# Attention prologue of a fused AdaLN + attention + MoE kernel: the second head's projections into PSUM banks 4 to 7, half of the third head's ahead of the first scores, the modulation rows' products first

## The chip, the cores and the metric

One Trainium2 chip, one core of it. The metric is device time in microseconds (us) from one launch to its end; lower is better. The inputs and outputs are fp32. A row of the trace gives times from the start of the profiled span.

## The reference, cut to what matters

```python
mod = (_silu(L0_c) @ L0_wmod).reshape(L0_c.shape[0], 6, 1, -1)
sa, ca, ga, sb, cb, gb = (mod[:, 0], mod[:, 1], mod[:, 2], mod[:, 3], mod[:, 4], mod[:, 5])
ga = (2 * (ga >= 0) - 1) * jnp.maximum(jnp.abs(ga), 0.25)   # the same for gb
h = _layernorm(x, axis=-1) * (1 + ca) + sa
x = x + ga * attention(h)          # 16 heads of 128, q and k RMS-normed, rope, softcap, causal
h = _layernorm(x, axis=-1) * (1 + cb) + sb
x = x + gb * moe(h)                # 64 experts, top 6, capacity 96, and a shared expert
```

x is 4 x 512 x 256 (batch, tokens, model). For each batch b and head n the attention makes q, k, v = h @ w, scores, their softmax, the product with v, and the output projection.

## The kernel before

Each engine has a program of its own, written out in order by hand; semaphores tie them together. The attention runs over 4 batches x 16 heads as 64 *periods*. In `period(b, p)` TensorE (PE) does: `scores(b, p)`; the transposes of the head before's output (`o_t`); the transposes of q and k of head p + 1 (`qk_t`); the projections q, k, v of head p + 2 (`qkv`); the output projection of head p - 1 (`proj`); and the product of the probabilities with v of head p (`pv`). So a head's projections are made two periods ahead of its scores. Every fp32 product of the projections and scores is made of three matmuls on split operands (high x high, high x low, low x high): `wh`, `wl` are the halves of a head's weights, `hth`, `htl` those of the transposed h, `qth`, `qtl`, `kth`, `ktl` those of q and k, `oth`, `otl` those of a head's output. ScalarE (ACT) makes the high halves, VectorE (DVE) the low ones.

PSUM has 8 banks. `qkv` writes banks 0 to 3 (one bank for 128 tokens, 384 columns: q, k, v); `qk_t` writes banks 2 and 3; `scores` write banks 4 to 6; `pv` writes banks 7 and 6; `proj` banks 4 and 5. The trace calls all of PSUM `ps` and most SBUF scratch `arena`.

After `qkv` of a head, and before PE can transpose that head's q, a chain over three engines has to run: ACT squares q and k (`take`, L593), DVE sums the squares (`squares_sum`, L861), GpSimd (POOL) raises the mean to the power -1/2 (`norms`, L500 and L502), DVE scales q (`q_scale`, L866). In `take` ACT also copies k and v out of PSUM; after it `weights_high` makes the next head's `wh`, which DVE's `weights_low` follows with `wl`.

Before the first period stands a prologue, with this order on PE: four columns of the modulation (L1282), the transposes of the normalised x (`h1_t`, L1297), `qkv(0, 0)` (24 matmuls, L1313 and L1325), `qk_t(0, 0)` (L1334, L1337), `qkv(0, 1)` (24 matmuls, L1325), `mod_rows` (the other four modulation vectors as rows: four fp32 products of a 128 x 4 stationary tile with 512 columns, which the trace shows as 8 records, L1289), a wait for the loads of the output weights and the gate, and then `period(0, 0)`. DVE copies the rows of `mod_rows` to SBUF (`rows_out`, L855), and reworks them in periods 0 and 1 (`rows_signed`, `rows_clamped`: sign, floor of 0.25). `scores(0, 0)` may write bank 6 only after that copy. The modulation weights for `mod_rows` come with the transfer issued at L337. All loads are issued from one queue (SP) at the start.

## Time and profile before

| | |
|---|---|
| median of 3 runs | 1035.48 us (1033.2 to 1037.18) |
| profiled execution, its own time | 1035.61 us |
| its span | 1033.8 us |
| PE busy | 979.1 us, 95% of the span |
| DVE, ACT, POOL busy | 692.0, 589.1, 383.3 us |
| mean granted clock of TensorE | 0.975 of full speed |

The span is what the trace covers; about 1.8 us of the execution's own time lie around it. A busy PE says that matmuls were in flight, not that they ran at full speed. TensorE has two clock levels, 1.2 and 2.4 GHz; the granted clock is given as a share of the higher.

### The profile page before, as it was taken

The numbers are of one execution on the slowest core, as the hardware profiler recorded it, in microseconds if no ns is written. First come the engines' busy times: TensorE is split into PE (matmuls) and PEld (weight loads), VectorE is DVE, ScalarE is ACT, GpSimd is POOL, SyncE is SP. The second block draws the span as 40 slices with busy tenths as digits, with TensorE's granted clock in tenths as the row PEclk, the third lists the DMA queues.
The fourth block names the chain that finished last, engine by engine and source line by source line (L and its number), as shares of the span: only waits on it lengthen the run. The fifth ranks groups of instructions, "written<-read, shape, count | busy, mean of one in ns | idle before, by whom it ended". The sixth has DMA issues, their size and how long they took to land.

```text
span 1033.8 us, 18164 instructions
## 1 busy us (share of the span) xinstructions
PE 979.1 (95%) x6301; PEld 874.2 (85%) x6301; DVE 692.0 (67%) x1783; ACT 589.1 (57%) x1093; POOL 383.3 (37%) x454
## 2 busy tenths in 40 slices
PE   4999999999999999999999999999989789999982
PEld 4899999999999999999999999999855356666661
DVE  3666666778788876878888686888568123324646
ACT  2666766766676676667666766666531024444420
POOL 3222222223322564332256432225624515555460
PEclk9999999999999999999999999999999899999985
DMA  9995000000100110010011004000261049999847
GB/s 349 333 325 209 0 0 1 1 2 14 45 1 1 49 49 33 5 53 1 2 48 39 24 2 145 2 1 17 100 204 36 26 121 309 311 313 306 235 46 243
DMA packets 71213, 103.42 MB, mean 100 GB/s; under 512 B 10237, under 2 KB 52352, under 8 KB 70750
## 3 DMA queue, kind: packets, MB, share of 16 engines
q1 hardware_dynamic: 45854, 74.62, 22.2%
q0 software_dynamic: 11808, 12.87, 6.1%
q10 hardware_dynamic: 13472, 14.90, 4.7%
q8 instruction: 46, 0.75, 0.3%
q14 instruction: 33, 0.27, 0.1%
HBM read 68.13 MB, written 40.88 MB: 105 GB/s over the span
## 4 chain that ended last, share of the span: by engine, by line
PE 88%; DVE 5%; DMA 3%; issue 2%; ACT 1%; POOL 0%; SPq 0%; ACTq 0%; POOLq 0%; DVEq 0%
PE ps L1325 26%; PE ps L1378 14%; PE ps L1351 12%; PE ps L1366 9%; PE ps L1531 7%; PE ps L1546 5%; PE ps L1358 3%; PE ps L1334 3%; PE ps L1415 3%; PE ps L1337 3%; PE ps L1484 1%; PE ps L1524 1%; DMA acc<-wos,arena 1%; DMA arena<-slot_rows 1%; PE ps L1538 1%
## 5 line engine op out<-in xcount | busy, mean ns | idle before, releaser
L617 ACT ACTIVATE prob<-ps,rn 128x512 f32<-128x512 f32 (+3 forms) x256 | 121.5, 528 | 113.8 <-PE ps L1351 107.0
L1325 PE MATMUL ps<-wl,hth 128*128 128x384 f32 x512 | 173.1, 338 | 0.0
L1325 PE MATMUL ps<-wh,htl 128*128 128x384 f32 x512 | 172.7, 337 | 0.0
L1325 PE MATMUL ps<-wh,hth 128*128 128x384 f32 x496 | 171.9, 347 | 0.0
L861 DVE TENSOR_REDUCE ss<-arena 128x8 f32<-128x1024 f32 x64 | 78.2, 1221 | 117.1 <-ACT arena L593 117.0
L1378 PE MATMUL ps<-vx,prob 128*128 128x129 f32 (+1 forms) x1280 | 153.4, 274 | 0.2 <-POOL prob L511 0.2
L1378 PEld LDWEIGHTS ps<-vx,prob 128*128 128x128 f32 x1280 | 148.2, 191 | 0.6 <-POOL prob L511 0.6
L593 ACT ACTIVATE arena<-ps 128x1024 f32<-128x1024 f32 x64 | 65.7, 1026 | 119.0 <-PE ps L1325 119.0
L508 POOL TENSOR_SCALAR_AFFINE_SELECT prob<-prob 128x384 f32<-128x384 f32 x64 | 35.6, 557 | 256.2 <-ACT prob L623 256.2
L572 POOL DMA_INDIRECT acc<-wos,arena x64 | 92.8, 1450 | 93.5 <-ACT wos L737 50.3
L517 POOL DMA_INDIRECT slot_rows<-pay,arena x96 | 99.8, 1039 | 43.2 <-issue 24.7
L502 POOL TENSOR_TENSOR rn<-rtmp,neghalf 128x8 f32<-128x8 f32 x64 | 105.4, 1648 | 5.3
L1325 PEld LDWEIGHTS ps<-wl,hth 128*128 128x128 f32 x512 | 97.5, 190 | 0.9 <-issue 0.9
L1325 PEld LDWEIGHTS ps<-wh,htl 128*128 128x128 f32 x512 | 97.2, 190 | 0.0
L1325 PEld LDWEIGHTS ps<-wh,hth 128*128 128x128 f32 x496 | 93.9, 189 | 0.1
L500 POOL TENSOR_SCALAR rtmp<-ss 128x8 f32<-128x8 f32 x64 | 12.6, 197 | 211.3 <-DVE ss L861 211.3
L1351 PE MATMUL ps<-qth,kth 128*128 128x512 f32 (+3 forms) x256 | 87.8, 343 | 0.0
L623 ACT ACTIVATE prob<-prob 128x1280 f32<-128x1280 f32 x64 | 83.7, 1308 | 0.0
L1351 PE MATMUL ps<-qtl,kth 128*128 128x512 f32 (+3 forms) x256 | 82.7, 323 | 0.0
L1351 PE MATMUL ps<-qth,ktl 128*128 128x512 f32 (+3 forms) x256 | 82.4, 322 | 0.0
L1208 DVE TENSOR_TENSOR xn<-ps,arena 96x176 f32<-96x176 f32 x64 | 21.5, 337 | 85.0 <-PE ps L1531 47.8
L891 DVE TENSOR_TENSOR arena<-ps,arena 128x512 f32<-128x512 f32 x118 | 75.6, 681 | 2.2 <-PE ps L1366 2.2
(208 smaller groups left out, 2237.8 us busy)
## 6 DMA issues: line engine op xcount, KB each, us to landing
acc<-pay SPq DMA_DIRECT2D x4, 2048.0 KB, 17.1
wge<-in_wgu SPq DMA_DIRECT2D x20, 352.0 KB
slot_rows<-pay SPq DMA_DIRECT2D x1, 6456.0 KB, 35.8
warena<-acc SPq DMA_DIRECT2D x12, 512.0 KB
arena<-slot_rows ACTq DMA_DIRECT2D x56, 100.9 KB
warena<-in_wqkv SPq DMA_DIRECT2D x1, 4992.0 KB, 20.6
arena<-in_wgu SPq DMA_DIRECT2D x14, 352.0 KB
late_t<-in_wd ACTq DMA_DIRECT2D x14, 192.0 KB
```

Source lines behind the costliest of these rows:

```text
L502: pool.tensor_tensor(rn[:, bass.ds(head(n), 1), :].squeeze(1), rtmp[:], neghalf[:], ALU.pow).then_inc(s["r_rdy"], 1)
L517: pool.indirect_dma_start(buf_d, bass.IndirectOffsetOnAxis(ap=sloti[:, i * K + k:i * K + k + 1], axis=0), pay[:, i, :], None, bounds_check ...
L572: pool.indirect_dma_start(acc_d[acc_of(e)], bass.IndirectOffsetOnAxis(ap=tokc[:, e % TR:e % TR + 1], axis=0), orow[e % ORING], None, bound ...
L617: act_(prob[:, OFF[j]:OFF[j] + w], sflat[:, OFF[j]:OFF[j] + w], ACT.Tanh, scale=rn[:, bass.ds(head(n), 1), TT + j:TT + j + 1].squeeze(1)). ...
L623: act_(prob[:, 0:1280], prob[:, 0:1280], ACT.Exp, scale=CAP).then_inc(s["expd"], 1)
L861: nc.vector.tensor_reduce(ss[:].rearrange("p (c i) -> p i c", c=2), sq, X, ALU.add).then_inc(s["ss_rdy"], 1)
L891: tt(ya, yp, ya, ALU.add).then_inc(s["y_added"], 1)
L1325: last = mm(ps[:, i, 0:3 * DH], hp[:, k, i * P:(i + 1) * P], wp[:, k, :], start=(k == 0 and m == 0), stop=(k == KC - 1 and m == 2))
L1351: last = mm(sflat[:, OFF[j]:OFF[j] + w], kp[:, j * P:(j + 1) * P], qp[:, T - w:T], start=(m == 0), stop=(m == 2))
L1366: last = mm(yps[:, i, :], op[:, i * P:(i + 1) * P], wp[:], start=(m == 0), stop=(m == 2))
L1378: last = mm(o, prob[:, c:c + P], vx[:, bass.ds((vslot(n) * TT + j) * (DH + 1), DH + 1)], start=(j == 0), stop=(j == i))
L1531: last = mm(ps[0:C, 1 + e % 2, 0:2 * M], xgt[:, e % 2, k, :], wgus[e % RING][:, k, :], start=(k == 0), stop=(k == KC - 1))
```

## The change

The prologue is put in another order, and the second head (`is_second`: batch 0, head 1) gets places of its own.

- PE: `mod_rows` moves from behind `qkv(0, 1)` to ahead of `qkv(0, 0)`. `qkv(0, 1)` writes banks 4 to 7 (`qbank`), so it no longer waits for head 0's q, k and v to be taken out of banks 0 to 3, and stands ahead of `qk_t(0, 0)`. It waits for the copy of the modulation rows (banks 6 and 7), and `scores(0, 0)` now waits until head 1's q and v have left banks 4 to 7. The first two token tiles of `qkv(0, 2)` stand ahead of `period(0, 0)`, the other two stay inside it. The wait for the output weights and the gate moves behind `period(0, 0)`.
- ACT: the high halves of the second head's weights (`second_high`) are made early, into the places of `oth` and `otl`, which are free then. `weights_high(0, 2)` follows `take(0, 0)`. `qk_high(0, 0)` moves inside `take(0, 1)`, behind its square.
- DVE: `second_low` makes the low halves into `kth` and `ktl`; `rows_out`, `rows_signed` and `rows_clamped` all come ahead of `squares_sum(0, 0)`; `squares_sum(0, 1)` comes ahead of `qk_t(0, 0)`.

No arithmetic is added or left out, except that one pass over a head's weights (high, and low) is two passes of half the size for head 1.

```diff
--- before.py
+++ after.py
@@ -236,6 +236,8 @@
         oth = hb("oth", [P, T])
         otl = hb("otl", [P, T])
         heads.close()
+        wh1 = [oth, otl]
+        wl1 = [kth, ktl]
         late_gu = [sb("late_h", [P, KC * T]), sb("late_l", [P, KC * T]), sb("late_wh", [P, KC * 3 * DH]), sb("late_wl", [P, KC * 3 * DH])]
         late_wd = [sb(f"late_t{i}", [P, T]) for i in range(6)]
 
@@ -318,6 +320,14 @@
 
         def vslot(n):
             return n % 4
+
+        def is_second(b, n):
+
+            return isinstance(b, int) and isinstance(n, int) and b == 0 and n == 1
+
+        def qbank(b, n):
+
+            return SB if is_second(b, n) else 0
 
         SB = 4
 
@@ -590,11 +600,14 @@
                 a.wait_ge(s["qkv_rdy"], cnt(b, n))
                 if some(cnt(b, n - 1)):
                     a.wait_ge(s["ss_rdy"], cnt(b, n - 1))
-                act_(sq, ps[:, 0:TT, 0:2 * DH].rearrange("p i (c d) -> p i c d", c=2), ACT.Square).then_inc(s["squared"], 1)
-                act_(kr, ps[:, 0:TT, DH:2 * DH], ACT.Copy).then_inc(s["k_copied"], 1)
+                q0 = qbank(b, n)
+                act_(sq, ps[:, q0:q0 + TT, 0:2 * DH].rearrange("p i (c d) -> p i c d", c=2), ACT.Square).then_inc(s["squared"], 1)
+                if is_second(b, n):
+                    qk_high(0, 0)
+                act_(kr, ps[:, q0:q0 + TT, DH:2 * DH], ACT.Copy).then_inc(s["k_copied"], 1)
                 dst = vx[:, bass.ds(vslot(n) * TT * (DH + 1), TT * (DH + 1))].rearrange("p (i d) -> p i d", i=TT)[:, :, 0:DH]
                 a.wait_ge(s["ones_rdy"], 1)
-                act_(dst, ps[:, 0:TT, 2 * DH:3 * DH], ACT.Copy).then_inc(s["v_copied"], 1)
+                act_(dst, ps[:, q0:q0 + TT, 2 * DH:3 * DH], ACT.Copy).then_inc(s["v_copied"], 1)
 
             def h_high(b):
 
@@ -606,9 +619,17 @@
 
             def weights_high(b, n):
 
-                if some(cnt(b, n - 1)):
+                if isinstance(b, int) and isinstance(n, int) and (b, n) == (0, 2):
+                    a.wait_ge(s["qkv_rdy"], cnt(0, 0))
+                elif some(cnt(b, n - 1)):
                     a.wait_ge(s["qkv_rdy"], cnt(b, n - 1))
                 act_(wh[:], wq[:, :, bass.ds(head(n), 1), :].squeeze(2), ACT.Copy).then_inc(s["wh_rdy"], 1)
+
+            def second_high():
+
+                for k in range(KC):
+                    ins = act_(wh1[k][:, 0:3 * DH], wq[:, k, 1, :], ACT.Copy)
+                ins.then_inc(s["wh_rdy"], 1)
 
             def cap(b, n):
 
@@ -679,13 +700,12 @@
 
             a.wait_ge(s["ld_wq0"], 16)
             weights_high(0, 0)
+            second_high()
             h_high(0)
             take(0, 0)
-            weights_high(0, 1)
+            weights_high(0, 2)
             a.wait_ge(s["g_rdy"], 4)
-            qk_high(0, 0)
             take(0, 1)
-            weights_high(0, 2)
             a.wait_ge(s["ld_wqkv"], 16)
             for p in range(2):
                 period(0, p)
@@ -819,6 +839,13 @@
                 v.wait_ge(s["wh_rdy"], cnt(b, n))
                 tt(wl[:], wq[:, :, bass.ds(head(n), 1), :].squeeze(2), wh[:].bitcast(F32), ALU.subtract).then_inc(s["wl_rdy"], 1)
 
+            def second_low():
+
+                v.wait_ge(s["wh_rdy"], 2)
+                for k in range(KC):
+                    ins = tt(wl1[k][:, 0:3 * DH], wq[:, k, 1, :], wh1[k][:, 0:3 * DH].bitcast(F32), ALU.subtract)
+                ins.then_inc(s["wl_rdy"], 1)
+
             def x_attended(b):
 
                 v.wait_ge(s["y_added"], 2 * cnt(b, H - 1))
@@ -863,7 +890,8 @@
             def q_scale(b, n):
                 v.wait_ge(s["r_rdy"], cnt(b, n))
                 v.wait_ge(s["v_copied"], cnt(b, n))
-                tt(qn, ps[:, 0:TT, 0:DH], rn[:, bass.ds(head(n), 1), 0:TT].squeeze(1).unsqueeze(2).to_broadcast([P, TT, DH]), ALU.mult).then_inc(s["q_scaled"], 1)
+                q0 = qbank(b, n)
+                tt(qn, ps[:, q0:q0 + TT, 0:DH], rn[:, bass.ds(head(n), 1), 0:TT].squeeze(1).unsqueeze(2).to_broadcast([P, TT, DH]), ALU.mult).then_inc(s["q_scaled"], 1)
 
             def qk_t(b, n):
                 v.wait_ge(s["qth_rdy"], cnt(b, n))
@@ -1022,8 +1050,6 @@
                     qk_t(b, p + 1)
                 if some(cnt(b, p - 1)):
                     wo_low(b, p - 1)
-                if not has_before(b) and isinstance(p, int) and p < 2:
-                    rows_signed() if p == 0 else rows_clamped()
                 if isinstance(p, int) and has_before(b):
                     if p == 1:
                         x_attended(b - 1)
@@ -1087,14 +1113,16 @@
             ts(g[:], g[:], qkws[:, 0:1], DH ** -0.5 / CAP, ALU.mult, ALU.mult).then_inc(s["g_rdy"], 1)
             v.wait_ge(s["g_rdy"], 4)
 
+            second_low()
+            rows_out()
+            rows_signed()
+            rows_clamped()
             squares_sum(0, 0)
+            weights_low(0, 2)
             q_scale(0, 0)
-            weights_low(0, 1)
+            squares_sum(0, 1)
             qk_t(0, 0)
-            squares_sum(0, 1)
-            rows_out()
             q_scale(0, 1)
-            weights_low(0, 2)
             v.wait_ge(s["consts"], 10)
             cp(trir[:], tri[:]).then_inc(s["pos_w"], 1)
             ts(onesr[:], tri[:], 0.0, 1.0, ALU.mult, ALU.add).then_inc(s["pos_w"], 1)
@@ -1297,9 +1325,15 @@
                         last = pe.transpose(ps[:, bank + k, i * P:(i + 1) * P], src[:, i, k * P:(k + 1) * P], ident[:])
                 last.then_inc(s["xt_ps"], 1)
 
-            def qkv(b, n):
-
-                before = cnt(b, n - 1)
+            def qkv(b, n, tiles=(0, TT)):
+
+                before = 0 if is_second(b, n) else cnt(b, n - 1)
+                q0 = qbank(b, n)
+                whs, wls = ([m[:, 0:3 * DH] for m in wh1], [m[:, 0:3 * DH] for m in wl1]) if is_second(b, n) else ([wh[:, k, :] for k in range(KC)], [wl[:, k, :] for k in range(KC)])
+                if is_second(b, n):
+                    pe.wait_ge(s["rows_sb"], 1)
+                if tiles == (0, 2):
+                    before = cnt(b, n - 2)
                 if some(before):
                     pe.wait_ge(s["v_copied"], before)
                     pe.wait_ge(s["q_scaled"], before)
@@ -1310,21 +1344,22 @@
                         for k in range(KC):
                             if i == 0:
                                 pe.wait_ge(s["h_high"], KC * (b + n // H) + k + 1)
-                            mm(ps[:, i, 0:3 * DH], hth[:, k, i * P:(i + 1) * P], wh[:, k, :], start=(k == 0), stop=False)
+                            mm(ps[:, q0 + i, 0:3 * DH], hth[:, k, i * P:(i + 1) * P], whs[k], start=(k == 0), stop=False)
                     pe.wait_ge(s["ht_rdy"], KC * (b + n // H + 1))
                 pe.wait_ge(s["wl_rdy"], cnt(b, n))
-                for i in range(TT):
+                for i in range(*tiles):
                     if i == 2 and some(before):
                         pe.wait_ge(s["qt_rdy"], before)
                     if i == 3 and some(before):
                         pe.wait_ge(s["kt_rdy"], before)
                     for k in range(KC):
-                        for m, (hp, wp) in enumerate(((hth, wh), (hth, wl), (htl, wh))):
+                        for m, (hp, wp) in enumerate(((hth, whs), (hth, wls), (htl, whs))):
                             if first and i < 2 and m == 0:
                                 continue
-                            last = mm(ps[:, i, 0:3 * DH], hp[:, k, i * P:(i + 1) * P], wp[:, k, :],
+                            last = mm(ps[:, q0 + i, 0:3 * DH], hp[:, k, i * P:(i + 1) * P], wp[k],
                                       start=(k == 0 and m == 0), stop=(k == KC - 1 and m == 2))
-                last.then_inc(s["qkv_rdy"], 1)
+                if tiles[1] == TT:
+                    last.then_inc(s["qkv_rdy"], 1)
 
             def qk_t(b, n):
 
@@ -1340,13 +1375,14 @@
             def scores(b, n):
                 pe.wait_ge(s["qt_rdy"], cnt(b, n))
                 pe.wait_ge(s["kt_rdy"], cnt(b, n))
+                if isinstance(b, int) and isinstance(n, int) and (b, n) == (0, 0):
+                    pe.wait_ge(s["v_copied"], cnt(0, 1))
+                    pe.wait_ge(s["q_scaled"], cnt(0, 1))
                 for j, w in ((0, 512), (1, 384), (3, 128), (2, 256)):
                     if j < 2 and some(cnt(b, n - 2)):
                         pe.wait_ge(s["y_added"], 2 * cnt(b, n - 2) + (j - 1))
                     if j == 2 and some(cnt(b, n - 1)):
                         pe.wait_ge(s["o_normed"], 2 * cnt(b, n - 1))
-                    elif j == 2:
-                        pe.wait_ge(s["rows_sb"], 1)
                     for m, (kp, qp) in enumerate(((kth, qth), (kth, qtl), (ktl, qth))):
                         last = mm(sflat[:, OFF[j]:OFF[j] + w], kp[:, j * P:(j + 1) * P], qp[:, T - w:T], start=(m == 0), stop=(m == 2))
                     if j != 1:
@@ -1438,7 +1474,7 @@
                         pe.wait_ge(s["ld_sh"], 32)
                     shared_up(p - (H - 2))
                 if not (is_last(b) and static and p >= H - 2):
-                    qkv(b, p + 2)
+                    qkv(b, p + 2, (2, TT) if static and b == 0 and p == 0 else (0, TT))
                 if static and p == 4 and has_before(b):
                     pe.wait_ge(s["h2s_rdy"], b)
                 if static and p == 5 and has_before(b):
@@ -1453,14 +1489,15 @@
                 pv(b, p)
 
             h1_t(0)
+            mod_rows()
             qkv(0, 0)
+            qkv(0, 1)
             qk_t(0, 0)
-            qkv(0, 1)
-            mod_rows()
+            qkv(0, 2, (0, 2))
+            period(0, 0)
             pe.wait_ge(s["ld_wo"], 16)
             pe.wait_ge(s["ld_gate"], 16)
-            for p in range(2):
-                period(0, p)
+            period(0, 1)
             with pe.Fori(2, SIDE) as p:
                 period(0, p)
             for b in range(B - 1):
```

PE's program at the start, where the prologue's large pieces stand (arena in the first row is the modulation weights, sc the activated condition; hth and wh are head 0's operands). Before:

```order
L1297 MATMUL ps<-ident,xn 128x128 [waits xn_rdy,consts]
...
L1313 MATMUL ps<-wh,hth 128x384 [waits h_high,wh_rdy]
...
L1334 MATMUL ps<-ident,arena 128x128 [waits v_copied,q_scaled]
...
L1325 MATMUL ps<-wh,hth 128x384 [waits wl_rdy,q_scaled,v_copied]
...
L1289 MATMUL ps<-arena,sc 4x512 [waits ld_wmod2]
...
L1351 MATMUL ps<-qth,kth 128x512 [waits qt_rdy,kt_rdy,ld_gate,ld_wo]
```

Of the changed kernel (oth and kth are here the high and low half of head 1's weights):

```order
L1325 MATMUL ps<-ident,xn 128x128 [waits xn_rdy,consts]
...
L1317 MATMUL ps<-arena,sc 4x512 [waits ld_wmod2]
...
L1347 MATMUL ps<-wh,hth 128x384 [waits h_high,wh_rdy]
...
L1359 MATMUL ps<-oth,hth 128x384 [waits wl_rdy,rows_sb]
...
L1369 MATMUL ps<-ident,arena 128x128 [waits v_copied,q_scaled]
...
L1359 MATMUL ps<-wh,hth 128x384 [waits wl_rdy,q_scaled,v_copied]
...
L1387 MATMUL ps<-qth,kth 128x512 [waits v_copied,q_scaled,kt_rdy,qt_rdy]
```

The rows' products stand ahead of everything of head 0, head 1's projections ahead of head 0's transposes, and the first scores wait for head 1's chain too.

DVE's program between the last small product of the prologue and head 1's scaling. Before:

```order
L861 TENSOR_REDUCE ss<-arena 128x4x2
L866 TENSOR_TENSOR arena<-ps,rn 128x512
L820 TENSOR_TENSOR wl<-warena,wh 128x768
L870 TENSOR_TENSOR qtl<-ps,qth 128x512
L872 SCALAR_TENSOR_TENSOR ktl<-ps,g,kth 128x512
L861 TENSOR_REDUCE ss<-arena 128x4x2
L855 COPY arena<-ps 4x1024
L866 TENSOR_TENSOR arena<-ps,rn 128x512
```

Of the changed kernel:

```order
L846 TENSOR_TENSOR kth<-warena,oth 128x384
L846 TENSOR_TENSOR ktl<-warena,otl 128x384
L882 COPY arena<-ps 4x1024
L1033 TENSOR_SCALAR arena<-arena 4x256
...
L1043 SCALAR_TENSOR_TENSOR arena<-arena 4x2x256
L888 TENSOR_REDUCE ss<-arena 128x4x2
L840 TENSOR_TENSOR wl<-warena,wh 128x768
L894 TENSOR_TENSOR arena<-ps,rn 128x512
L888 TENSOR_REDUCE ss<-arena 128x4x2
L898 TENSOR_TENSOR qtl<-ps,qth 128x512
L900 SCALAR_TENSOR_TENSOR ktl<-ps,g,kth 128x512
L894 TENSOR_TENSOR arena<-ps,rn 128x512
```

The copy and the rework of the modulation rows moved ahead of head 0's sum of squares, and head 1's sum ahead of head 0's low halves.

## Rows read from the trace of the kernel before

**Rows 1.** The page: busy time of each engine

```profile
PE 979.1 (95%) x6301; PEld 874.2 (85%) x6301; DVE 692.0 (67%) x1783; ACT 589.1 (57%) x1093; POOL 383.3 (37%) x454
```

**Rows 2.** PE's waits from 40 to 700 us: total, times, longest

```profile
PE ps L1378 <- POOL prob L511: 0.2, 1, 0.2
```

**Rows 3.** PE's waits from 0 to 46 us

```profile
PE ps L1282 <- DMA arena<-in_wmod: 6.5, 1, 6.5
PE ps L1334 <- DVE arena L866: 5.2, 1, 5.2
PE ps L1313 <- ACT hth L605: 2.0, 1, 2.0
```

**Rows 4.** PE's timeline: start, length, line, operands, idle before

```profile
10.17 1.94 PE L1297 MATMUL ps<-ident,xn 128*128 128x128 f32 x8
14.10 1.95 PE L1313 MATMUL ps<-wh,hth 128*128 128x384 f32 x4 [1.99 <-ACT hth L605]
...
18.41 0.52 PE L1325 MATMUL ps<-wh,hth 128*128 128x384 f32 x1
18.73 0.52 PE L1325 MATMUL ps<-wl,hth 128*128 128x384 f32 x1
...
19.69 0.38 PE L1325 MATMUL ps<-wl,hth 128*128 128x384 f32 x1
...
26.50 1.06 PE L1334 MATMUL ps<-ident,arena 128*128 128x128 f32 x4 [5.18 <-DVE arena L866]
...
32.17 0.33 PE L1325 MATMUL ps<-wh,hth 128*128 128x384 f32 x1
32.35 0.33 PE L1325 MATMUL ps<-wl,hth 128*128 128x384 f32 x1
...
33.31 3.60 PE L1289 MATMUL ps<-arena,sc 128*4 128x512 f32 x8
36.84 0.50 PE L1351 MATMUL ps<-qth,kth 128*128 128x512 f32 x1
```

**Rows 5.** The chain that ended last: head 0's scaling

```profile
21.36 1.03 ACT arena L593
...
22.48 1.23 DVE ss L861
...
24.07 1.65 POOL rn L502
...
25.75 0.70 DVE arena L866
```

**Rows 6.** SP's timeline and L337's own view: issue, then DMA to landing

```profile
3.10 0.61 SPq L337 DMA_DIRECT2D arena<-in_wmod  x1
...
DMA to landing us min/median/max: 10.3/10.3/10.3
```

**Rows 7.** PE's timeline at the end; a window there (clock third from the end)

```profile
1000.48 13.99 PE L1573 MATMUL ps<-pay,warena 64*128 64x256 f32 x32 [3.65 <-DVE pay L1263]
...
1010.00:1012.00 2.00, 2.00 (x6) 1.63 (x5) 0.00 (x0) 0.00 (x0) 0.00 (x0) 0.50 1.07 378
```

**Rows 8.** Windows: the clock (third number from the end) after the wait

```profile
27.00:28.00 1.00, 1.00 (x7) 1.00 (x6) 0.31 (x1) 0.34 (x1) 0.00 (x0) 0.50 1.17 377
30.00:31.00 1.00, 1.00 (x8) 1.00 (x7) 0.00 (x0) 0.00 (x0) 0.00 (x0) 0.99 1.00 426
```

**Rows 9.** DVE's timeline

```profile
22.48 1.22 DVE L861 TENSOR_REDUCE ss<-arena 128x8 f32<-128x1024 f32 x1 [6.43 <-ACT arena L593]
...
36.95 1.21 DVE L855 COPY arena<-ps 4x1024 f32<-4x1024 f32 x1 [1.25 <-PE ps L1289]
...
52.84 1.01 DVE L1015 SCALAR_TENSOR_TENSOR arena<-arena 4x512 f32<-4x512 f32 x1
```

**Rows 10.** The chain that ended last: the first period

```profile
40.22 0.71 ACT kth L642
...
44.42 2.50 PE ps L1378 x20
```

## The prediction

> **What bounds the kernel now.** I read the page's busy times first: PE is busy for 979.1 of 1033.8 us, DVE for 692.0, ACT for 589.1 [rows 1]. So PE is the engine to watch, and the question is where it waits. The view of waits, asked for PE alone, answers it: from 40 to 700 us PE waited once, for 0.2 us [rows 2]. What the change touches lies ahead of that, and there PE waited three times: 6.5 us for the first modulation weights, 2.0 us for the first high half of h, and 5.2 us for head 0's scaled q [rows 3]. Since PE is gapless behind the prologue, a microsecond won or lost before the first scores comes out at the end nearly whole: the time at which `scores(0, 0)` starts, 36.84 us [rows 4], is the number that the whole prediction turns on. I call it S.
>
> The timeline of PE shows a second thing: its speed. A 128x384 matmul follows the one before it after 0.32 us at 18.41 us (half speed) and after 0.18 us at 32.17 us (full speed) [rows 4]. The change of pace stands at 19.69 us, 5.6 us after the projections started at 14.10. The wait of 5.2 us cost more than itself: the granted clock is 0.50 at 27 us and back at 0.99 in the stretch from 30 us, 3.5 us after PE resumed at 26.50 [rows 8, 4]. (For the first 19 us the spacing, not the granted clock, tells the level: 384 columns in 0.32 us are 1.2 GHz.)
>
> **The change part by part.**
>
> *The rows' products, moved.* Before, the 8 records take 33.31 to 36.84, 3.5 us at full speed [rows 4]. Now they stand behind the transposes, which end at 12.1 us (10.17 + 1.94), and wait for the transfer issued at 3.10, which lands 10.3 us later, at 13.4 us [rows 4, 6]. There PE runs at half speed. The price at 1.2 GHz comes from the kernel's end, where 32 records of 256 columns take 13.99 us at granted clock 0.50, 0.437 us each [rows 7]; records of 512 columns are twice that, and 8 of them 7.0 us. So they end at 20.4 us, where `qkv(0, 0)` had begun at 14.10: the start is 6.3 us later, against 3.5 us taken out further on. That is a loss of 2.8 us, unless the clock rises while they run.
>
> *Does it?* This decides the case. At the kernel's end PE ran 14 us without a gap on stationary tiles of 64 rows, and the clock stayed at 0.50 all the time [rows 7]. From 14.10 us and from 26.50 us, on tiles of 128 x 128, it rose after 5.6 and 3.5 us. The stationary tile of the rows' products has 4 columns of 128; it is further from the tiles that brought the clock up than the tile that didn't. So I take it that the clock stays at 1.2 GHz through them, and keep the other answer as a rival.
>
> *`qkv(0, 0)`.* 24 matmuls, starting cold at 20.4. Before, they took 7.2 us (14.10 to 21.3) with the clock rising 5.6 us in. If it rises 3.5 us in, as after the later wait, 2.1 us of half speed (6.5 matmuls of 0.32) become 6.5 x 0.175 = 1.1 us, so 6.3 us. I take the middle, 6.8: end at 27.2 (26.7 to 27.6).
>
> *`qkv(0, 1)` in the 5.2 us wait.* It now follows at once, warm: 24 x 0.175 = 4.2 us, end at 31.4. Its operands are early: two half passes of high weights cost ACT at most twice the 1.03 us of its 1024-column square [rows 5], and PE now asks for ACT's high half of h 6.3 us later than before; the low ones lie in DVE's idle 6.43 us ahead of its first sum [rows 9]. Its wait for the copied rows ends at 20.4 + 1.2 = 21.6. The PE wait it fills is not the end of the wait: `qk_t(0, 0)` may start 5.2 us after 27.2 (the chain is 1.03, 1.23, 1.65 and 0.70 us and the hand-overs [rows 5]), so at 32.4, with 1.0 us of idle PE left. Since PE no longer stands for 5.2 us in a row, the second fall of the clock goes. What that fall cost, 26.50 to 30.0 at half speed, is 3.5 / 2 = 1.75 us.
>
> *The wait comes back behind head 1.* `scores(0, 0)` needs banks 4 to 7 free, and they are free when head 1's chain is through. That is another 5.2 us, after 31.4: S = 36.6. In it PE has 8 transposes (1.94 us at half speed [rows 4], so 1.0) and 12 matmuls of head 2 (2.1) to do; they end at 32.4 + 3.1 = 35.5, and PE idles 1.1 us. On ACT, the high half of head 0's k and the copies of head 1's k and v now stand between head 1's square and the release of v. At 0.71 us each, as that high half [rows 10], they follow the transposes' end at 33.4 and are done at 35.5; the power of head 1 is ready 4.4 us after 31.4 (as 25.72 came after 21.3 [rows 5]), at 35.8. So the chain sets S, and they don't, by 0.3 us. On DVE, `weights_low(0, 2)` now stands ahead of `q_scale(0, 0)`. It waits for ACT's square, two copies and a 768-column pass (at most 1.03 + 1.42 + 1.03 = 3.5) and is no longer than the 1.23 of a sum: 4.7 us at the very most against 4.4, so at worst 0.3 us on head 0's chain. The wait for the output weights and the gate, now behind period 0, held PE for nothing before: the rows' products run up to 36.84 [rows 4].
>
> *Half of head 2 early.* It takes 2.1 us out of period 0, but does that move anything? In period 0, `pv(0, 0)` starts 7.6 us after the scores (36.84 to 44.42) and the chain through it is not PE's but tanh, high halves, the load of the exponential's table, exponential and mask [rows 10]. In the chain of what ended last, PE's own projections of that period do not appear. So the 2.1 us turn into idle PE, in front of tile 2 (which needs the low half of head 1's q) or of `pv`. I cost the piece at a gain of 0.1 us, since head 2's chain can start a little sooner, and at no more than 0.3 us, the size of the wait that remained ahead of `pv`.
>
> *DVE's rows first.* The copy is 1.21 us and the longest of the five reworks 1.01 [rows 9]; even at that all six are under 6.3 us, and they run from 20.4 to 26.7 at the latest. Head 0's square is done at 27.2 + 1.1 = 28.3. In periods 0 and 1 DVE is the lighter by the same work, and PE did not wait for it there [rows 2]: nothing.
>
> **The sum.** S goes from 36.84 to 36.6, and 0.1 us comes from period 0: a gain of 0.3 us. Over the two bounds of the clock's rise, S is 36.1 to 37.0, a gain of 0.8 to a loss of 0.1. Against the profiled execution's own time of 1035.61 that is 1035.3; this execution is 0.13 us above the median of 1035.48, so I say 1035.2. Three runs of one kernel lie 4.0 us apart, which is far more.
>
> **The rivals.**
>
> *The clock rises inside the rows' products.* What speaks for it is that PE is busy without a gap from 13.4 on. With the rise 3.5 to 5.6 us in, half (3.5 of 7.0) to four fifths of them are done cold and they end at 18.7 to 19.7; `qkv(0, 0)` is warm, 4.2 + 0.2, so 23.0 to 24.0; `qkv(0, 1)` 27.2 to 28.2; S = 32.4 to 33.4. (DVE, with its rows done 6.3 us after 18.7 at the latest, might cost 0.9 of that.) Gain 3.4 to 4.4, in the middle 3.9, with period 0 4.0: 1031.5 us. The Trainium skill, page "TensorE: Matmul & The Clock Gate", section "What's actually happening", says that the gate follows how busy PE has lately been, whatever it works on; by that rule this rival is the forecast. The stretch of 14 us above does not agree with it.
>
> *Slower: the clock stays low past the projections.* PE now has idle stretches of 1.0 and 1.1 us where it was gapless after 26.50. If PE stays at half speed until the first scores are done, `qkv(0, 0)` takes 7.7 (S + 0.9), `qkv(0, 1)` 7.7 instead of 4.2 (+ 3.5), and the scores, of 3840 columns or ten times 384, 10 x 0.145 more (+ 1.5): 5.9 us against the gain of 0.3, 1041 us. It decides "slower" only from a rise behind S; a rise at the end of `qkv(0, 1)` is a loss of 4.1 us and still no difference. Against it: both rises before came 3.5 and 5.6 us after 128 x 128 matmuls began.
>
> *The transfer is late.* Each us by which the second modulation weights land after 13.4 moves S by one; before, PE asked for them at 33.3 and they had 20 us of slack. To lose over 0.5% they must land 5.5 us later. Nothing in the issue order changes, so I give it little.
>
> *Nothing is gained since the wait only moves.* This is near the forecast: without the clock effect, S would be within 0.3 us of before by coincidence of a loss of 2.8 and the gains of the filled wait.
>
> **How the numbers follow.** 0.5% is 5.2 us, about what a measurement of this kernel can tell from no change, and more than the forecast or the first rival reach. Chances: forecast 0.55; clock rising inside the rows' products 0.33; clock low for longer 0.05; late transfer 0.02; something unseen 0.05, either way. Faster by over 0.5% takes the first rival's far end and a before that ran high: 0.08. Slower by over 0.5%: 0.06. Within: 0.86. The range reaches down to the first rival (1031.5) less 1 us of the runs' scatter, and up by the forecast's loss plus the 2 us by which runs lie over their median: 1030.5 to 1038.0. The forecast's own is 1033.0 to 1037.5.
>
> **What would show it.** In the changed kernel's trace: the rows' products start at 13.4 and end at 20.4, each record starting 0.87 us after the last (0.43 us in the later ones would be the rival); spacing of 0.32 us in the first half of `qkv(0, 0)`; no granted clock of 0.50 after it; PE idle about 1.0 us ahead of head 0's transposes, 1.1 ahead of the scores, and some 2.3 in all within period 0; S at 36.6. Wrong it would be by a clock that rises early, or by a wait in ACT's or DVE's new order that I took to be covered.

## The result and the profile after

| | before | changed |
|---|---|---|
| median of 5 runs | 1036.81 us (1033.2 to 1037.67) | 1028.23 us (1027.1 to 1029.77) |
| profiled execution, its own time | 1035.61 us | 1028.68 us |
| its span | 1033.8 us | 1026.8 us |
| mean granted clock | 0.975 | 0.977 |

The ratio is 0.9929, 95% interval 0.9915 to 0.9943: the changed kernel is faster by 0.7%, some 7.4 us. The forecast was 1035.2 us with a range of 1030.5 to 1038.0, and a chance of 0.08 for a gain over 0.5%. It was wrong.

The page of the changed kernel, its span and its busy times, answers to [rows 1]:

```profile
span 1026.8 us, 18168 instructions
...
PE 975.8 (95%) x6301; PEld 870.5 (85%) x6301; DVE 692.2 (67%) x1784; ACT 589.1 (57%) x1094; POOL 384.9 (37%) x454
```

PE is busy for 3.3 us less (979.1 to 975.8) on the same work, so part of the gain must be pace, not waiting. PE's waits of the changed kernel from 0 to 42 us (in total, times, longest; from 42 to 700 us there is none) answer to [rows 3]:

```profile
PE ps L1310 <- DMA arena<-in_wmod: 6.4, 1, 6.4
PE ps L1317 <- DMA arena<-in_wmod: 1.5, 1, 1.5
PE ps L1359 <- DVE qtl L898: 1.4, 1, 1.4
PE ps L1387 <- DVE arena L894: 1.1, 1, 1.1
PE ps L1369 <- DVE arena L894: 0.9, 1, 0.9
PE ps L1414 <- POOL prob L521: 0.8, 1, 0.8
```

The wait of 5.2 us is gone, and that of 2.0 us for h has become one of 1.5 us for the modulation weights; 0.9, 1.1, 1.4 and 0.8 have come. Where the time came from stands in PE's timeline of the changed kernel, which answers to [rows 4] (start, length, operands, idle before):

```profile
10.09 1.94 PE L1325 MATMUL ps<-ident,xn 128*128 128x128 f32 x8
13.52 4.98 PE L1317 MATMUL ps<-arena,sc 128*4 128x512 f32 x8 [1.49 <-DMA arena<-in_wmod]
18.43 0.98 PE L1347 MATMUL ps<-wh,hth 128*128 128x384 f32 x4
19.25 0.34 PE L1359 MATMUL ps<-wl,hth 128*128 128x384 f32 x1
...
22.72 0.33 PE L1359 MATMUL ps<-oth,hth 128*128 128x384 f32 x1
...
27.99 0.66 PE L1369 MATMUL ps<-ident,arena 128*128 128x128 f32 x4 [0.95 <-DVE arena L894]
...
32.29 0.47 PE L1387 MATMUL ps<-qth,kth 128*128 128x512 f32 x1 [1.08 <-DVE arena L894]
...
36.70 0.41 PE L1359 MATMUL ps<-wh,hth 128*128 128x384 f32 x1 [1.38 <-DVE qtl L898]
...
39.83 2.50 PE L1414 MATMUL ps<-vx,prob 128*128 128x129 f32 x20 [0.79 <-POOL prob L521]
```

The rows' products took 4.98 us, not 7.0 (all at 1.2 GHz) and not 3.5 (all at 2.4). Within them the pace doubled: cold for x us and warm for the rest is x + (7.0 - x) / 2 = 4.98, so x = 3.0. `qkv(0, 0)` follows at full pace from its first record, 18.43 to 22.72, 4.3 us. S, the start of the first scores, is 32.29.

From one span to the other it is 7.0 us. S accounts for 4.55 (36.84 to 32.29), the stretch from S to `scores(0, 2)` for 0.36 (21.23 to 20.87), so 4.9 are there by the third head. Of the rest, 0.9 stands ahead of the last output projection (its idle time is 2.39 us before and 1.46 after), and 1.0 between the second layer's transposes and the first expert (67.4 and 66.35 us). The further traces below tell against the change as the cause of either. The idle time ahead of that projection is 1.46 us in all of them, variants of the kernel before included. The second stretch takes 56.8 or 58.5 us and nothing else, for variants of either kernel (before: 56.8 in the copy, 58.5 with the rows' products moved; changed: 58.5 and 56.8 in two copies). So I take the last 2 us of the pair of profiles for scatter; where its two values come from stands with the copies below. Those executions were on other chips, where the kernel before takes some 1026 us; each ratio below is to runs of the kernel before on the same chip.

### The profile page after: what moved, and what is told of

It is laid out like the page before. It is cut to its first block, busy times and chain, and to the rows that moved or that the text cites. A ratio compares the mean times of both kernels' runs of the same rounds, so it can differ in the third digit from the quotient of the medians.

```text
span 1026.8 us, 18168 instructions
## 1 busy us (share of the span) xinstructions
PE 975.8 (95%) x6301; PEld 870.5 (85%) x6301; DVE 692.2 (67%) x1784; ACT 589.1 (57%) x1094; POOL 384.9 (37%) x454
## 4 chain that ended last, share of the span: by engine, by line
PE 88%; DVE 5%; DMA 4%; issue 1%; ACT 1%; POOL 0%; SPq 0%; ACTq 0%; POOLq 0%; DVEq 0%
PE ps L1359 25%; PE ps L1414 14%; PE ps L1387 12%; PE ps L1402 9%; PE ps L1568 7%; PE ps L1583 5%; PE ps L1451 3%; PE ps L1394 3%; PE ps L1369 3%; PE ps L1372 3%; PE ps L1521 1%; DMA acc<-wos,arena 1%; DMA warena<-acc 1%; PE ps L1561 1%; DMA arena<-in_wmod 1%
## 5 line engine op out<-in xcount | busy, mean ns | idle before, releaser
L1359 PE MATMUL ps<-wh,hth 128*128 128x384 f32 x488 | 168.4, 345 | 1.4 <-DVE qtl L898 1.4
L1359 PE MATMUL ps<-wl,hth 128*128 128x384 f32 x504 | 169.0, 335 | 0.0
L1359 PE MATMUL ps<-wh,htl 128*128 128x384 f32 x504 | 168.8, 335 | 0.0
L604 ACT ACTIVATE arena<-ps 128x1024 f32<-128x1024 f32 x64 | 65.7, 1026 | 116.7 <-PE ps L1359 116.7
L582 POOL DMA_INDIRECT acc<-wos,arena x64 | 95.6, 1493 | 89.4 <-ACT wos L757 57.6
L1359 PEld LDWEIGHTS ps<-wl,hth 128*128 128x128 f32 x504 | 94.8, 188 | 0.9 <-issue 0.9
L1359 PEld LDWEIGHTS ps<-wh,htl 128*128 128x128 f32 x504 | 94.6, 188 | 0.0
L1359 PEld LDWEIGHTS ps<-wh,hth 128*128 128x128 f32 x488 | 91.8, 188 | 1.6 <-issue 1.6
L510 POOL TENSOR_SCALAR rtmp<-ss 128x8 f32<-128x8 f32 x64 | 12.6, 197 | 205.3 <-DVE ss L888 205.3
```

The costliest lines, as they stand in the source:

```text
L582: pool.indirect_dma_start(acc_d[acc_of(e)], bass.IndirectOffsetOnAxis(ap=tokc[:, e % TR:e % TR + 1], axis=0), orow[e % ORING], None, bound ...
L1359: last = mm(ps[:, q0 + i, 0:3 * DH], hp[:, k, i * P:(i + 1) * P], wp[k], start=(k == 0 and m == 0), stop=(k == KC - 1 and m == 2))
```

## The experiments

**The rows' products first, and nothing else.** In the kernel before, moved on PE as shown; DVE's copy of the rows moves ahead of the first sum of squares with them:

```diff
             h1_t(0)
+            mod_rows()
             qkv(0, 0)
             qk_t(0, 0)
             qkv(0, 1)
-            mod_rows()
```

> The kernel before with one part of the change: the rows' products (and their copy on DVE) ahead of qkv(0,0); the rest as before. Theory 1 (the early rows carry the gain: they fill PE's wait for h and bring the clock up before the projections): they run 13.5 to 18.4 us, qkv(0,0) is warm and ends at 22.7, the wait of 5.2 us stays, first scores at 22.7 + 5.2 + 0.9 + 4.2 = 33.0 us if the clock stays up in the wait, 34.7 if it falls: 3.8 or 2.1 us below the kernel before. Theory 2 (the filled wait carries it): first scores at 36 us or later, under 1 us gained.

Measured: 1028.19 against 1025.75 us, ratio 1.0017 (1.0007 to 1.0028). Its timeline (PE), and two windows of it (the clock is the third number from the end):

```profile
13.85 5.02 PE L1289 MATMUL ps<-arena,sc 128*4 128x512 f32 x8 [1.85 <-DMA arena<-in_wmod]
...
28.36 1.12 PE L1334 MATMUL ps<-ident,arena 128*128 128x128 f32 x4 [5.10 <-DVE arena L866]
...
41.24 1.12 PE L1334 MATMUL ps<-ident,arena 128*128 128x128 f32 x4 [3.18 <-DVE arena L866]
```

```profile
28.00:29.00 1.00, 0.65 (x3) 0.65 (x4) 1.00 (x2) 0.00 (x0) 0.00 (x0) 0.50 1.25 450
...
41.00:42.00 1.00, 0.76 (x4) 0.76 (x5) 1.00 (x3) 0.00 (x0) 0.00 (x0) 0.50 1.06 312
```

The products take 5.02 us here too, so the early rise of the clock doesn't need the other edits. But alone the move gains nothing; it loses 0.17%. S is 35.98, later than the 33.0 to 34.7 of the first theory, and from there it goes worse. Before, the products stood between `qkv(0, 1)` and its scaled q and filled that chain; with them gone, PE waits 3.18 us for it inside period 0, and the clock falls a second time. `scores(0, 2)` starts at 61.71 us, against 58.07 and 58.89 in the two traces of the kernel before.

**The rows' products late.** In the changed kernel they go behind the first half of `qkv(0, 2)`, with the waits that banks 6 and 7 then need; DVE copies and reworks the rows where it did before.

```diff
             h1_t(0)
-            mod_rows()
             qkv(0, 0)
             qkv(0, 1)
             qk_t(0, 0)
             qkv(0, 2, (0, 2))
+            mod_rows()
             period(0, 0)
```

> The changed kernel with the rows' products behind the first half of qkv(0,2), as late as before, and everything else of the change kept. Theory 1: qkv(0,0) starts cold at 14.1 and ends at 21.3, qkv(0,1) at 25.5, head 1's chain at 30.7, the rows' products 3.6 us behind it: first scores at 34.3 us, 2 us above the changed kernel. Theory 2 (only the filled wait counts): within 0.5 us of the changed kernel's 32.3.

Measured: 1020.87 against 1025.75 us, 0.9953 (0.9935 to 0.9970). PE's timeline:

```profile
14.01 1.96 PE L1345 MATMUL ps<-wh,hth 128*128 128x384 f32 x4 [1.75 <-ACT hth L618]
...
30.18 3.59 PE L1317 MATMUL ps<-arena,sc 128*4 128x512 f32 x8 [1.05 <-issue]
33.70 0.50 PE L1387 MATMUL ps<-qth,kth 128*128 128x512 f32 x1
```

The products cost 3.59 us warm and start after a stretch idle of 1.05 us that is there in either place. S is 33.70, between the two theories. With them first it is 32.29, 33.45 and 33.91 in three profiles of the changed kernel. So by the traces their place is worth 1.4 us at most and may be worth nothing; the two ratios' intervals (0.9935 to 0.9970 here, 0.9921 to 0.9961 for the copy below) overlap. Most of the gain is there without that edit.

**Half of head 2 not early.** The changed kernel without the `qkv(0, 2, (0, 2))` ahead of period 0:

```diff
             qk_t(0, 0)
-            qkv(0, 2, (0, 2))
             period(0, 0)
...
-                    qkv(b, p + 2, (2, TT) if static and b == 0 and p == 0 else (0, TT))
+                    qkv(b, p + 2)
```

> The changed kernel with qkv(0,2) whole inside period 0. Theory 1, as in the prediction: the first scores stay at 32.3 us, pv(0,0) stays at 39.8 since tanh, table load, exponential and mask set it; within 0.3 us of the changed kernel. Theory 2 (the half is worth its 2.1 us): pv(0,0) at 41 us or later.

Measured: 1024.01 against 1025.75 us, 0.9987 (0.9971 to 1.0004). Some three quarters of the gain go with 12 matmuls that only change places. PE's timeline and windows of this kernel:

```profile
32.93 0.77 PE L1387 MATMUL ps<-qth,kth 128*128 128x512 f32 x1 [3.20 <-DVE arena L894]
```

```profile
30.00:31.00 1.00, 0.00 (x0) 0.00 (x0) 1.00 (x3) 1.00 (x3) 0.77 (x2) 0.88 1.04 442
...
36.00:37.00 1.00, 1.00 (x6) 1.00 (x6) 0.00 (x0) 0.92 (x3) 0.00 (x0) 0.50 1.04 400
...
38.00:39.00 1.00, 1.00 (x8) 1.00 (x7) 0.56 (x1) 0.98 (x3) 0.00 (x0) 1.00 1.03 238
```

S is 32.93, as the forecast's step would have it: the half doesn't move the chain. But PE stands for 3.20 us ahead of it instead of 1.08, the clock falls in that wait (the scores' first record lasts 0.77 us, not 0.47) and is low for 6.8 us. From S to `scores(0, 2)` it takes 23.23 us instead of 20.87, 2.36 us more. The timed difference to the changed kernel is larger, some 4.7 us (0.9987 against 0.9941, each to the kernel before on its own chip); what makes up the rest no run shows.

**The same with work that computes nothing.** Twelve matmuls into a free bank take the half's place in the kernel above (added work, its results unused):

```diff
             qk_t(0, 0)
+            for _ in range(12):
+                mm(ps[:, 0, 0:3 * DH], hth[:, 0, 0:P], hth[:, 1, 0:3 * DH], start=True, stop=True)
```

> The changed kernel without the early half of qkv(0,2), and in its place 12 matmuls of 128x384 whose result nobody reads. Without the half, the clock fell in a wait of 3.2 us and pv(0,0) started 9.5 us after the first scores instead of 7.6. Theory 1 (the early half is worth its holding of the clock, not its work): pv(0,0) starts 7.6 us after the first scores, as in the changed kernel. Theory 2 (its work counts): 9.5 us again, or over 8.5.

Measured, one execution: 1019.31 us beside a median of 1026.01. PE's timeline and a window:

```profile
33.13 0.47 PE L1387 MATMUL ps<-qth,kth 128*128 128x512 f32 x1 [1.09 <-DVE arena L894]
...
40.68 2.50 PE L1414 MATMUL ps<-vx,prob 128*128 128x129 f32 x20 [0.35 <-POOL prob L521]
```

```profile
36.00:37.00 1.00, 1.00 (x8) 1.00 (x7) 0.29 (x1) 1.00 (x3) 0.00 (x0) 1.00 1.05 406
```

The clock stays up, and `pv(0, 0)` comes 7.55 us after S, as in the changed kernel (7.54), where it was 9.48 with the half late. What the half of head 2 is worth is that it keeps PE busy; that it is done early is worth 0.2 us at most (from S to `scores(0, 2)` 21.06 us here, 20.87 in the changed kernel).

**Tiles of 64 rows.** Each of the rows' products is made of two on the first 64 rows, so half of each sum is left out and the count of records is doubled:

```diff
-  last = mm(ps[0:B, 6 + h, :], sc[:, k, :], wmods[:, k, ...], ...)
+  for r in range(2):
+      last = mm(ps[0:B, 6 + h, :], sc[0:64, k, :], wmods[0:64, k, ...], ...)
```

> The changed kernel with each of the four rows' products replaced by two over the first 64 rows only (the other half of each sum is left out): twice the columns streamed, stationary tiles of 64 x 4. It asks whether the rows of a tile decide if the clock comes up. Theory 1 (tiles of 64 rows don't bring it up, as in the 14 us at the kernel's end): 16 records at 0.87 us, 13.5 to 27.5 us, and qkv(0,0) starts cold; first scores at 43 us or later. Theory 2 (being busy is enough): spacing falls from 0.85 to 0.43 us about 3 us in, the products end at 22 us, first scores at 35.8.

Measured, one execution: 1031.72 us beside a median of 1025.75. PE's timeline, and a window of it:

```profile
13.47 13.81 PE L1318 MATMUL ps<-arena,sc 64*4 64x512 f32 x16 [1.24 <-DMA arena<-in_wmod]
27.21 1.65 PE L1348 MATMUL ps<-wh,hth 128*128 128x384 f32 x4
28.65 0.52 PE L1360 MATMUL ps<-wl,hth 128*128 128x384 f32 x1
...
31.92 0.33 PE L1360 MATMUL ps<-wh,hth 128*128 128x384 f32 x1
```

```profile
30.00:31.00 1.00, 1.00 (x5) 1.00 (x4) 0.91 (x2) 0.00 (x0) 0.00 (x0) 1.00 1.00 426
```

16 records in 13.81 us are 0.863 each, the 0.87 of 1.2 GHz, to the end. That it is the clock, and not a slower kind of matmul, shows in what follows on 128 x 128 tiles: records of 0.52 us, every 0.32 us, until the pace changes at 31.5, 4.3 us after these began; from there on they last 0.33. In 13.8 us without a gap the clock did not rise. The granted clock reads 1.00 in the window, where the spacing is that of 1.2 GHz: ahead of its first change in a trace it can't be used.

**The rows' products twice.** The control for it, the same count of records with whole tiles (added work, the second pass writes what the first did):

```diff
-                for h in range(2):
+                for h in (0, 1, 0, 1):
```

> The changed kernel with the rows' products made twice in a row (the second pass writes the same result). Theory 1 (their 128-row tiles bring the clock up, and it then stays up under them): the second pass takes 3.5 us, first scores 3.5 us later than in the changed kernel, at 35.8 to 36.5. Theory 2 (the rise at 16 us came from the transposes ahead, and tiles of 4 columns don't hold the clock): it falls again in them, first scores at 38 us or later.

Measured, one execution: 1021.3 us beside 1026.1. PE's timeline:

```profile
12.70 7.98 PE L1317 MATMUL ps<-arena,sc 128*4 128x512 f32 x16 [0.56 <-DMA arena<-in_wmod]
```

As many records of as many columns, on 128 rows instead of 64: 7.98 us instead of 13.81. The rise comes 2.0 us after the start (14.0 cold, 7.0 warm), and a whole extra pass leaves S at 34.45, within 0.6 us of the changed kernel's latest.

**Both kernels again.** Unchanged copies on another chip, the changed one on a third too.

> The kernel before, unchanged, as a control: a second profile of it. Of the changed kernel's gain, 5.0 us lie ahead of the third head's scores and 2.0 us behind the attention (0.9 us at the last output projection, 1.0 us in the shared expert's stretch). Theory A (those 2.0 us are scatter of the executions or of the chip): on this chip the stretch from the last head's scores to its output projection takes 13.0 us, as in the four kernels profiled here, and 58.5 us from the transposes of h2 to the first expert. Theory B (they come with the kernel's layout): 13.9 us for the first. The first scores start between 35.1 and 37.0 us, by where the clock rises and falls.

> The changed kernel, unchanged, on the chip on which its variants were timed. Theory A: first scores at 32.3 to 33.0 us (the rows' products start 13.5 to 14.1, by the landing of their weights), the gain over the kernel before is the prologue's 4 to 5 us, a ratio of 0.995 to 0.996. Theory B: the whole 7 us again, 0.993.

> The changed kernel once more, beside the version with two more edits, for their difference on one chip. The first scores start at 32.3 to 33.9 us, by the place of the clock's rise in the rows' products; ratio to the kernel before 0.994.

Measured: before 0.9995 (0.9983 to 1.0008); changed 0.9941 (0.9921 to 0.9961) and 0.9943 (0.9931 to 0.9955), 1020.54 against 1026.01 us. The traces differ from the first ones. The changed kernel's timeline on the second chip:

```profile
13.68 6.47 PE L1317 MATMUL ps<-arena,sc 128*4 128x512 f32 x8 [1.66 <-DMA arena<-in_wmod]
...
33.91 0.47 PE L1387 MATMUL ps<-qth,kth 128*128 128x512 f32 x1 [1.11 <-DVE arena L894]
```

Here the rise came 5.9 us after their start instead of 3.0. Over all profiles with the products first, on whole tiles and made once, they took 4.17 to 6.47 us. The kernel before varies as well; its copy's timeline and windows:

```profile
26.15 1.11 PE L1334 MATMUL ps<-ident,arena 128*128 128x128 f32 x4 [5.17 <-DVE arena L866]
```

```profile
28.00:29.00 1.00, 1.00 (x5) 1.00 (x5) 0.81 (x2) 0.69 (x1) 0.00 (x0) 0.50 1.30 453
...
31.00:32.00 1.00, 1.00 (x4) 1.00 (x4) 0.00 (x0) 0.00 (x0) 0.00 (x0) 0.50 1.00 426
...
33.00:34.00 1.00, 1.00 (x7) 0.88 (x6) 0.00 (x0) 0.00 (x0) 0.00 (x0) 1.00 0.85 327
```

After the same wait the clock was low for 6.8 us in all, where [rows 8] had it back at 30. Its S is 37.65.

The copies also show where the two lengths of the stretch behind the attention come from. PE's timeline and a window of the first trace of the changed kernel, then of the copy on the second chip:

```profile
753.44 0.40 PE L1402 MATMUL ps<-woh,oth 128*128 128x256 f32 x1 [1.46 <-DVE otl L905]
754.00:755.00 1.00, 1.00 (x7) 1.00 (x6) 0.97 (x2) 0.00 (x0) 0.00 (x0) 0.50 1.05 351
764.65 1.06 PE L1325 MATMUL ps<-ident,pay 128*128 128x128 f32 x8 [1.12 <-DVE pay L873]
```

```profile
766.28 1.26 PE L1325 MATMUL ps<-ident,pay 128*128 128x128 f32 x8 [2.63 <-DVE pay L873]
768.00:769.00 1.00, 1.00 (x3) 0.77 (x3) 0.00 (x0) 0.60 (x1) 0.00 (x0) 0.50 0.60 210
```

In the first the clock falls at the last output projection, the work behind it is slow, and it fills the wait for the transposes' operand but for 1.12 us. In the copy the clock stays up there, PE waits 2.63 us, and the clock falls behind that wait: the stretch is 1.7 us longer. In all nine traces with 58.5 us this wait is 2.6 to 2.7 us, and in all other traces 1.0 to 1.4.

**The wait filled in the kernel before.** 24 matmuls into a free bank in the 5.2 us (added work, unused):

```diff
             qkv(0, 0)
+            for _ in range(24):
+                mm(ps[:, 5, 0:3 * DH], hth[:, 0, 0:P], hth[:, 1, 0:3 * DH], start=True, stop=True)
             qk_t(0, 0)
```

> The kernel before with 24 matmuls of 128x384 added, whose result nobody reads, between qkv(0,0) and qk_t(0,0), in PE's wait of 5.2 us (4.2 us of extra work, no work moved). Theory 1 (a part of what the wait costs is the clock, which fell in it in both profiles of the kernel before and came back 3.5 to 5.9 us after PE resumed): no granted clock of 0.50 after 20 us, first scores 1.7 to 3 us sooner, at 34.6 to 35.2 us, and the kernel 1.5 to 3 us faster than before though it does more. Theory 2 (the wait costs only its own length): first scores at 36.8 to 37.6 as before, no difference in time.

Measured: 1023.39 against 1026.01 us, 0.9977 (0.9968 to 0.9986). PE's timeline:

```profile
21.40 4.33 PE L1458 MATMUL ps<-hth 128*128 128x384 f32 x24
26.74 0.66 PE L1334 MATMUL ps<-ident,arena 128*128 128x128 f32 x4 [1.01 <-DVE arena L866]
...
32.03 3.60 PE L1289 MATMUL ps<-arena,sc 128*4 128x512 f32 x8
36.09 0.47 PE L1351 MATMUL ps<-qth,kth 128*128 128x512 f32 x1 [0.46 <-DMA wos<-in_wo]
```

The kernel gets 2.4 us faster by doing more. That is the cost of the clock's fall, measured apart from the wait: from `qk_t(0, 0)` to the rows' products it takes 5.29 us, and 6.81 and 7.98 in the two traces of the kernel before. The last row shows something else: with the clock held up the scores are due at 35.63, and wait 0.46 us for the loads. (The trace names the output weights; the gate's load, issued at 23.44, lands 12.6 us later, at 36.0.) In the kernel before the gate's load lands at 35.1 (23.56 + 11.5) and PE asks for it at 36.84. So the wait that "held PE for nothing" was 1.8 us from holding it.

**The wait for the loads put back.** The changed kernel with the two waits ahead of period 0 again:

```diff
             qkv(0, 2, (0, 2))
+            pe.wait_ge(s["ld_wo"], 16)
+            pe.wait_ge(s["ld_gate"], 16)
             period(0, 0)
-            pe.wait_ge(s["ld_wo"], 16)
-            pe.wait_ge(s["ld_gate"], 16)
             period(0, 1)
```

> The changed kernel with PE's wait for the output weights and the gate back ahead of period 0. The prediction costed the moving of this wait at nothing. Theory 1 (nothing only while the scores start late: the weights land at 35 to 36 us, after the changed kernel's first scores): the first scores start at 35 to 36.1 us with an idle of 2 to 4 us ahead of them, in which the clock may fall; 2 to 4 us slower than the changed kernel. Theory 2 (nothing, as predicted): first scores at 32.3 to 33.9, no difference.

Measured: 1026.60 against 1025.71 us, 1.0005 (0.9992 to 1.0018). PE's timeline and two windows:

```profile
36.70 0.76 PE L1387 MATMUL ps<-qth,kth 128*128 128x512 f32 x1 [4.59 <-DMA gates<-in_gate]
```

```profile
34.00:35.00 1.00, 0.00 (x0) 0.00 (x0) 0.00 (x0) 0.00 (x0) 0.00 (x0) 1.00 0.91 344
...
37.00:38.00 1.00, 1.00 (x3) 0.81 (x3) 0.00 (x0) 0.00 (x0) 0.00 (x0) 0.50 1.08 398
```

The gate's load lands at 36.7 us. PE stands 4.59 us instead of 1.09, so S is 36.70 and 3.5 us late. The clock falls too, and from S to `scores(0, 2)` it takes 23.06 us, 2.2 more. The whole gain is gone. Moving this wait is the edit without which the others show nothing.

**Two further steps.** The modulation weights issued ahead of head 0's weights, and ACT's table for the exponential loaded at the end of the prologue; each alone, and both:

```diff
-            sp.dma_start(wq[:, :, 0:nf, :], wqkv[:, :, 0:nf, :]).then_inc(s["ld_wq0"], 16)
             sp.dma_start(wmods[:, :, 2 * D:6 * D], wmod[:, :, 2 * D:6 * D]).then_inc(s["ld_wmod2"], 16)
+            sp.dma_start(wq[:, :, 0:nf, :], wqkv[:, :, 0:nf, :]).then_inc(s["ld_wq0"], 16)
...
             take(0, 1)
+            act_(warm[:], neghalf[:, 0:1], ACT.Exp)
```

> The changed kernel with only the rows' weights loaded ahead of the first heads' weights. The rows' products start at 12.1 us without a wait; first scores at 31.1 to 31.7, as in the two profiles with both edits, and pv(0,0) 7.6 us after them.

> The changed kernel with only the exponential's table loaded early. pv(0,0) starts 6.6 us after the first scores instead of 7.6, without PE's wait ahead of it; first scores at 32.3 to 33.9 as in the changed kernel. Of this 1.0 us, 0.5 may come back in period 1, where PE then waits for head 2's scaling (0.5 us in both profiles of the kernel with both edits).

> The changed kernel with two more edits: the rows' weights are loaded ahead of the first heads' weights, and a one-element exponential behind take(0,1) loads its table in ACT's idle time. Theory 1: the rows' products start at 12.1 us, end at 17.7; first scores at 31.6; pv(0,0) no longer waits for the 1.28 us of the table and starts 6.7 us after the scores (bounded by the projections' second half), at 38.3: 1.5 us below the changed kernel. Theory 2: the first heads' weights come too late instead and the first scores stay at 32.3 or later; then only the table's 0.8 us are won.

> The rows' weights loaded first and the exponential's table loaded early, again, with more rounds. Theory 1 (the third head's scores 1.5 to 3 us sooner, as the profiles had it): 0.0015 to 0.003 below the changed kernel's ratio. Theory 2 (lost in the scatter of the clock's phase): no difference that five rounds show.

Measured: the loads alone, one execution, 1018.29 us; the table alone, one execution, 1021.93 (beside 1025.71). Both: 0.9939 (0.9920 to 0.9959) on one chip, where the changed kernel had 0.9941, and 0.9930 (0.9918 to 0.9942), 1018.88 us, on another, where the changed kernel had 0.9943 (0.9931 to 0.9955). PE's timeline of the two single kernels, the loads first:

```profile
12.12 5.34 PE L1317 MATMUL ps<-arena,sc 128*4 128x512 f32 x8
...
31.23 0.47 PE L1387 MATMUL ps<-qth,kth 128*128 128x512 f32 x1 [1.09 <-DVE arena L894]
```

```profile
45.64 0.66 PE L1370 MATMUL ps<-ident,arena 128*128 128x128 f32 x4 [0.50 <-DVE arena L895]
```

The swap takes the 1.5 us wait ahead of the rows' products away. The early table brings `pv(0, 0)` 0.9 us nearer to S (6.59 us behind it instead of 7.54), but a wait of 0.50 us comes one period on (the second fence), and at `scores(0, 2)` 0.3 us of it is left (20.61 against 20.87). Both together have the lowest median of the kernels that were timed more than once; the intervals of this and the changed kernel overlap, so that it beats the changed kernel is likely and not shown. It beats the kernel before.

## Why the prediction was wrong, step by step

**The step that failed: "I take it that the clock stays at 1.2 GHz through them".** Along the chain of the prologue:

| | forecast | measured |
|---|---|---|
| rows' products start | 13.4 | 13.52 |
| they take (to the next start) | 7.0 | 4.9 |
| `qkv(0, 0)` | 6.8 | 4.3 |
| `qkv(0, 1)` | 4.2 | 4.3 |
| idle ahead of `qk_t(0, 0)` | 1.0 | 0.95 |
| transposes and half of head 2 | 3.1 | 3.2 |
| idle ahead of the scores | 1.1 | 1.08 |
| S | 36.6 | 32.29 |

Two rows hold the error: 2.1 us in the products and 2.5 in `qkv(0, 0)`, and both are the clock's. The reading behind it was of [rows 7]: a stationary tile of 64 x 128 had left the clock low, one of 128 x 128 had raised it, and I called 128 x 4 nearer to the first because of its few columns. The pair of 16 records tells it apart: with four columns and 128 rows the pace doubled after 2.0 us, with four columns and 64 rows it did not in 13.8. So for tiles of four columns it is the rows that count, and I had chosen the columns. (Whether the rows are also what kept the clock low on the 64 x 128 tiles of [rows 7] was not run; each of the two kernels was traced once.) The first rival had the mechanism and nearly the S (32.4 to 33.4, measured 32.29, 33.45 and 33.91); its 1031.5 us was still 3.3 too high.

By the Trainium skill, page "TensorE: Matmul & The Clock Gate", section "What's actually happening", the clock follows how busy PE has been, whatever it works on, and how many matmuls run cold varies between runs of one kernel. The changed kernel agrees with both (4.98 and 6.47 us for the same records). The 64-row tiles, 13.81 us without a gap and at half speed, do not agree with the first.

**Right.** The new waits: 0.95 and 1.08 us on the chain, and in period 0 1.38 + 0.79 = 2.17 against 2.3. That the chain sets S, not ACT's or DVE's new order: both waits are released by DVE's scaling (L894). That the transfer would land in time: off by 0.1 us.

**Right about its work, wrong about its price: half of head 2.** "So the 2.1 us turn into idle PE" is so in where the chain runs, but the step priced the piece at 0.1 us, and at 0.3 at most. Without it the kernel loses 2.36 us from S to `scores(0, 2)` (23.23 against 20.87), and the dummy matmuls win 2.17 of them back. The forecast had said that the second fall of the clock goes, and had not asked which of the edits holds it up. One of them was this.

**Right at the old start, wrong at the new one: the wait for the loads, costed at nothing.** At S = 36.6 it costs nothing, and the forecast had S there. In the trace where it was put back the chain would have let S be 33.2; the wait costs 3.5 us of standing, and 2.2 by the clock. The two errors hung together, since only an S that moves makes the wait matter.

**The fall of the clock in the 5.2 us wait, "3.5 / 2 = 1.75 us".** The size was near that of one execution (6.81 against 5.29 us to the rows' products, 1.5 us). Filled, the wait gave 2.4 us with the extra work still in; in the second profile of the kernel before 6.0 us of half speed follow the wait (26.15 to 32.16), which is 3.0.

**"For nothing" the rival that the wait only moves.** It does move, from 5.2 us to 0.95 + 1.08 + 1.38 + 0.79 = 4.2, only 1.0 us less. What changed besides is that the clock fell in none of its pieces.

**What stays open.** The traces give 4.9 us ahead of the third head in the first pair and 4.1 in the second; the timed gains are 5.8 us (0.9943 of 1026.0) to 7.4 us (0.9929 of 1036.8). One execution of each kernel is traced, and the clock's rise moves by some us between executions, in the kernel before too. The stretch behind the last transposes, 56.8 or 58.5 us, scatters besides, by the clock: in the second pair the changed kernel has the long one and the kernel before the short one, and the two traced executions lie only 2.1 us apart (1024.49 and 1022.36), though the changed one was 4.1 ahead at the third head. Its time is 2.5 us above its median of 1019.9. Scatter of this size would cover the 1 to 2.5 us that are missing, but no run separates it. Why the chips differ by 10 us behind the attention was not tried.

## What to carry to other kernels

Price an idle stretch of TensorE twice, by its length and by the clock that it may drop behind it, and before calling a filler worthless remove it in thought and ask whether the stretch that opens is of a length that dropped the clock elsewhere in the trace. A wait costed at nothing holds only for the start time that it was costed at: whenever a change may shorten the path, list what is then late next, load landings above all. And where two measured cases share a property (tiles of 64 x 128 and 128 x 128 have the same columns), they say nothing of what changing it does (a tile of 128 x 4).

## What the runs showed of the hardware that was not expected

- Under stationary tiles of 128 rows and 4 columns TensorE rose to 2.4 GHz 1.3 to 5.9 us after they began (8 records in 4.17 to 6.47 us; in the case of 1.3 us transposes had run right up to them). Under tiles of 64 rows and 4 columns it stayed at 1.2 GHz for 13.8 us.
- Idle stretches of 3.2, 4.6 and 5.2 us in the prologue dropped the clock for 3.4 to 6.8 us in all, and so did the nine of 2.6 to 2.7 us behind the attention; stretches of 0.95 to 1.88 us in the prologue did not (1.88 in the kernel with both further steps). But short stretches are not safe everywhere: ahead of the last output projection two of them, 1.18 and 1.46 us with four transposes between, were followed by 1.2 GHz in the first trace of the changed kernel and not in its copy.
- 24 matmuls whose results nobody reads made a kernel faster by 0.23% (0.9977, 0.9968 to 0.9986).
- Ahead of its first change in a trace the granted clock of the records can't be used: it reads 1.00 up to some 19 us in the kernel before, and up to 31 us with the tiles of 64 rows, while the spacing of the matmuls is that of 1.2 GHz.
